# An RNN feeding an LSTM on one core: LSTM step 1's recurrent product in fp16 halves, and the first TensorE instructions in another order

## The reference

```python
x = x + rnn(x, h0=cond_1024)    # h = tanh(h @ Wh + x_t @ Wx + b)
x = x + lstm(x, h0=cond_1024)   # a = x_t @ Wx + h @ Wh + b, 2048 columns: i, f, o, g
                                # c = sigmoid(f)*c + sigmoid(i)*tanh(g);  h = sigmoid(o)*tanh(c)
```

## Time and profile before

| | |
|---|---|
| median of 3 runs | 835.24 us |
| the profiled execution's own time | 836.42 us |
| its span in the trace | 834.6 us |
| TensorE (PE) busy | 823.8 us, 99% |
| VectorE (DVE) busy | 651.4 us, 78% |
| ScalarE (ACT) busy | 608.1 us, 73% |
| GpSimd (POOL) busy | 336.1 us, 40% |

### The profile page before, as it was taken

The page is one execution under the profiler, slowest core; times in us unless marked ns, Lnnn a source line. Parts: engine busy times, 40 slices in busy tenths (PEclk is TensorE's granted clock), DMA queues, the critical chain, the costliest instruction groups (busy, mean ns, idle before and its releaser), DMA issues.

```text
span 834.6 us, 52074 instructions
## 1 busy us (share of the span) xinstructions
PE 823.8 (99%) x22610; PEld 613.4 (73%) x22610; DVE 651.4 (78%) x1797; ACT 608.1 (73%) x1632; POOL 336.1 (40%) x693
## 2 busy tenths in 40 slices
PE   8999999999999999999999999999999999999997
PEld 5556555677777777777777777777777777777786
DVE  4798778877988878878787887878878787767764
ACT  3986576776777677777877778787787878777752
POOL 1422466845544344343434434343343434333320
PEclk9999999999999999999999999999999999999999
DMA  8711101110011111111111111111111101010001
GB/s 304 257 53 28 29 16 29 29 29 23 11 29 30 29 36 30 34 42 38 47 30 34 25 42 41 35 45 35 30 29 42 42 21 37 17 32 23 13 11 28
DMA packets 54580, 36.21 MB, mean 43 GB/s; under 512 B 9788, under 2 KB 52944, under 8 KB 53072
## 3 DMA queue, kind: packets, MB, share of 16 engines
q1 hardware_dynamic: 54096, 32.78, 14.2%
q10 hardware_dynamic: 256, 0.11, 0.0%
HBM read 19.21 MB, written 8.39 MB: 33 GB/s over the span
## 4 chain that ended last, share of the span: by engine, by line
PE 92%; DVE 3%; DMA 2%; issue 1%; ACT 1%; SPq 0%; POOL 0%; ACTq 0%; DVEq 0%; POOLq 0%
PE ps_l L1631 36%; PE ps_l L1726 29%; PE ps_r L1854 9%; PE ps_l L1673 4%; PE ps_pk L1837 3%; PE ps_r L1874 2%; PE ps_end L1837 2%; PE ps_l L1645 2%; DMA whl_raw<-in_L_cond_Wh 2%; PE ps_l L1665 1%; PE ps_r L1785 1%; PE ps_r L1796 1%; DMA wxr_raw<-in_L_cond_Wx 1%; PE ps_l L1618 0%; PE ps_l L1608 0%
## 5 line engine op out<-in xcount | busy, mean ns | idle before, releaser
L598 POOL TENSOR_TENSOR xb<-xb,h_l 128x128 f32<-128x128 f32 x127 | 58.2, 458 | 370.2 <-DVE h_lo L1437 368.0
L1726 PE MATMUL ps_l<-whl_raw,wxl_raw 128*32 128x256 f16 x3816 | 132.0, 273 | 0.0
L1631 PE MATMUL ps_l<-whl_hi,hT_hi 128*32 128x512 f16 x1888 | 122.6, 379 | 0.3 <-DVE hT_hi L1421 0.3
L1631 PE MATMUL ps_l<-whl_hi,hT_lo 128*32 128x512 f16 x1888 | 122.7, 379 | 0.0
L1631 PE MATMUL ps_l<-whl_lo,hT_hi 128*32 128x512 f16 x1888 | 122.5, 379 | 0.0
L1726 PE MATMUL ps_l<-wxl_hi,wxl_raw 128*32 128x256 f16 x2544 | 116.0, 273 | 0.0
L1726 PEld LDWEIGHTS ps_l<-whl_raw,wxl_raw 128*32 128x32 f16 x3816 | 102.2, 97 | 2.5 <-issue 0.4
L1631 PEld LDWEIGHTS ps_l<-whl_hi,hT_lo 128*32 128x32 f16 x1888 | 50.9, 97 | 51.1
L1631 PEld LDWEIGHTS ps_l<-whl_lo,hT_hi 128*32 128x32 f16 x1888 | 50.9, 97 | 51.1
L1009 ACT ACTIVATE gates<-ps_l,g_products 128x256 f32<-128x256 f32 x115 | 54.0, 469 | 41.8 <-PE ps_l L1631 41.6
L1726 PEld LDWEIGHTS ps_l<-wxl_hi,wxl_raw 128*32 128x32 f16 x2544 | 68.6, 97 | 17.5 <-issue 0.2
(11 more groups left out here) (265 smaller groups left out, 1929.6 us busy)
## 6 DMA issues: line engine op xcount, KB each, us to landing
xb<-in_x SPq DMA_DIRECT2D x128, 64.0 KB, 2.1
out<-xb SPq DMA_DIRECT2D x124, 64.0 KB, 1.9
whl_raw<-wxl_lo SPq DMA_DIRECT2D x160, 32.0 KB, 2.3
whl_raw<-in_L_cond_Wh SPq DMA_DIRECT2D x4, 1024.0 KB, 6.4
wxl_raw<-in_L_cond_Wx SPq DMA_DIRECT2D x4, 1024.0 KB, 7.0
wxr_raw<-in_L_cond_Wx SPq DMA_DIRECT2D x1, 1024.0 KB, 6.3
whr_raw<-in_L_cond_Wh SPq DMA_DIRECT2D x1, 1024.0 KB, 8.4
wxl_raw<-in_L_cond_b SPq DMA_DIRECT2D x1, 256.0 KB, 3.5
```

What stands on the lines that cost most here:

```text
L598: nc.gpsimd.tensor_tensor(xb[g % NX][:, t, :], xb[g % NX][:, t, :], h_l[s % 2][:, :], ALU.add).then_inc(out_done, 1)
L1631: last = nc.tensor.matmul(ps_l[s % 4][quarter(j), :], (hT_hi, hT_lo)[h_part][:, k, :], gate_slice(whl[w_part][k], j), start=False, stop=(h ...
L1726: last = nc.tensor.matmul(at[quarter(j), :], stationary, weights[:, j, :, :], start=False, stop=(y_part == 1 and k == 1), skip_group_check ...
```

## The change

LSTM step 1's recurrent product goes from float32 to fp16 halves (N0 from 2 to 1). With it `hidden(0)` writes halves; step 1's bias seed becomes the scaled one, as a second `seed_l` in ScalarE's tick 6; its input is scaled (`y_scale(0)` takes three steps, 128 x 384); the scale is taken off again at its gates. Its three groups of products stand in the order high-high, low hidden times high weights, high hidden times low weights, and the last group waits for each chunk of low halves by itself. TensorE's list begins with fourteen fills in a row; the bias products stand behind them, three of the four behind RNN input product 0. In tick 4 `turn_peaks` stands behind RNN input product 5 and `spread_peaks` behind `step_0_recurrent`. No other table or loop is touched.

```diff
--- before.py
+++ after.py
@@ -18,7 +18,7 @@
 NX = 8
 
 
-N0 = 2
+N0 = 1
 S1 = 5
 G1 = S1 // TG
 
@@ -761,7 +761,7 @@
 
 
             act.wait_ge(bias_mm, 1)
-            nc.scalar.activation(bias_r, ps_l[2][:, 0:P], ACT.Copy).then_inc(bias_done, 1)
+            nc.scalar.activation(bias_r, ps_pk[:, 0:P], ACT.Copy).then_inc(bias_done, 1)
 
             def bias_of_l():
                 act.wait_ge(bias_mm, 2)
@@ -1136,7 +1136,8 @@
                 if k in Y_SCALE_AT:
                     y_scale(Y_SCALE_AT[k])
                 if k == LAG - 1:
-                    seed_l(N0)
+                    for s in range(N0, 3):
+                        seed_l(s)
                 for of, chunk in W_HIGH_LATE_AT.get(k, []):
                     weight_high(of, chunk)
                 if k < LAG and k in R_HIGH_AT:
@@ -1602,8 +1603,8 @@
 
             def step_1_input(k):
 
-                pe.wait_ge(bias_done, 2)
-                pe.wait_ge(yT_done, 2)
+                pe.wait_ge(l_seeded, 1)
+                pe.wait_ge(y_scaled, 1)
                 for j in range(J):
                     last = nc.tensor.matmul(ps_l[1][quarter(j), :], yT[0][:, k, 1, :], gate_slice(wxl_raw[k], j),
                                             start=False, stop=False, skip_group_check=True)
@@ -1621,17 +1622,19 @@
                     return
                 m = s + 1 - N0
                 if m == 1:
-                    pe.wait_ge(w_split[OF_H], J)
+                    pe.wait_ge(w_high[OF_H], J)
                 pe.wait_ge(lstm_hT_hi, m)
                 for h_part, w_part in parts:
                     if h_part == 1:
                         pe.wait_ge(lstm_hT_lo, m)
                     for k in range(J):
+                        if m == 1 and w_part == 1:
+                            pe.wait_ge(w_split[OF_H], k + 1)
                         for j in range(J):
                             last = nc.tensor.matmul(ps_l[s % 4][quarter(j), :], (hT_hi, hT_lo)[h_part][:, k, :],
                                                     gate_slice(whl[w_part][k], j), start=False,
-                                                    stop=(h_part == 1 and k == J - 1), skip_group_check=True)
-                if parts[-1] == (1, 0):
+                                                    stop=((h_part, w_part) == parts[-1] and (1, 0) in parts and k == J - 1), skip_group_check=True)
+                if (1, 0) in parts:
                     last.then_inc(lstm_mm, 1)
 
             def recurrent_halves(s):
@@ -1907,39 +1910,34 @@
                 return last
 
             pe.wait_ge(ident_done, 1)
-            fill(ps_l[3], 3)
-            fill(ps_l[0], 2)
-            fill(ps_end, 1)
+            fill(ps_l[3], 4)
+            fill(ps_l[0], 4)
+            fill(ps_end, 2)
+            fill(ps_l[2], 4).then_inc(banks_written, 1)
             pe.wait_ge(spread_j_done, 1)
             pe.wait_ge(s_bias_r, DMA)
-            nc.tensor.matmul(ps_l[2][:, 0:P], spread_j, bias_rows_r, start=True, stop=True).then_inc(bias_mm, 1)
-
-            for r in (0, 1):
-                nc.tensor.matmul(ps_r[r][:, 0:P], spread_j, bias_rows_r, start=True, stop=True)
-            pe.wait_ge(s_bias_l, DMA)
-            nc.tensor.matmul(ps_l[1][:, :], spread_j, bias_rows_l, start=True, stop=True).then_inc(bias_mm, 1)
-            pe.wait_ge(bias_done, 1)
-            fill(ps_l[2], 6).then_inc(banks_written, 1)
+            nc.tensor.matmul(ps_r[0][:, 0:P], spread_j, bias_rows_r, start=True, stop=True)
             product_r(0)
             for k in range(END):
                 if k - LAG == S1:
                     recurrent_l(S1, ((0, 0), (0, 1)))
-                elif 1 <= k - LAG < S3:
+                elif k - LAG == 1:
+                    recurrent_l(1, ((0, 0), (1, 0), (0, 1)))
+                elif 1 < k - LAG < S3:
                     recurrent_l(k - LAG)
                 elif S3 <= k - LAG:
                     recurrent_halves(k - LAG)
                 if k == LAG - 1:
                     step_0_input(0)
                 if k == 0:
-                    fill(ps_pk, 2)
+                    nc.tensor.matmul(ps_pk[:, 0:P], spread_j, bias_rows_r, start=True, stop=True).then_inc(bias_mm, 1)
+                    nc.tensor.matmul(ps_r[1][:, 0:P], spread_j, bias_rows_r, start=True, stop=True)
+                    pe.wait_ge(s_bias_l, DMA)
+                    nc.tensor.matmul(ps_l[1][:, :], spread_j, bias_rows_l, start=True, stop=True).then_inc(bias_mm, 1)
                 if k < LAG:
                     recurrent_r(k)
                 if k == LAG - 1:
                     step_0_input(1)
-                if k == SCALE_AT[OF_H]:
-                    pe.wait_ge(w_peaked[OF_H], J)
-                    pe.wait_ge(r_step, 1)
-                    turn_peaks(EXCHANGE[OF_H], slice(0, J))
                 if k == SCALE_AT[OF_X]:
                     pe.wait_ge(w_peaked[OF_X], J)
                     pe.wait_ge(x_peaked, BATCHES[0][1])
@@ -1958,14 +1956,19 @@
                 if k < LAG:
                     next_product_r(k + 1)
                 if k == SCALE_AT[OF_H]:
-                    spread_peaks(EXCHANGE[OF_H], J)
+                    pe.wait_ge(w_peaked[OF_H], J)
+                    pe.wait_ge(r_step, 1)
+                    turn_peaks(EXCHANGE[OF_H], slice(0, J))
                 if k == R_SCALE_AT:
+                    pe.wait_ge(bias_done, 1)
                     pe.wait_ge(r_peaked, 2)
                     turn_peaks(EXCHANGE_R, slice(R_PEAK, R_PEAK + 2))
                 if k - 1 == R_SCALE_AT:
                     spread_peaks(EXCHANGE_R, 2)
                 if k in STEP_0_AT:
                     step_0_recurrent(STEP_0_AT[k])
+                if k == SCALE_AT[OF_H]:
+                    spread_peaks(EXCHANGE[OF_H], J)
                 if k == LAG - 1:
                     step_0_input(2)
                     step_1_input(0)
@@ -1975,9 +1978,9 @@
                     step_0_input(3)
                     step_1_input(3)
 
-                if N0 <= k - LAG + 1 < S1:
+                if 2 <= k - LAG + 1 < S1:
                     product_f32(k - LAG + 1, (2, 3))
-                if N0 <= k - LAG + 2 < S1:
+                if 2 <= k - LAG + 2 < S1:
                     product_f32(k - LAG + 2, (0, 1))
                 if k - LAG == S1:
                     product_l(S1 + 1, ((0, 0),))
```

## The result

The changed kernel takes 837.04 us (median of 15 runs, 836.64 to 838.58), the kernel before 835.93 us in the same comparison (15 runs). The ratio is 1.0014, 95% interval 1.0007 to 1.0020: about 1.1 us slower, where 1.0 us was forecast, and less than the 0.2% that would count as a change. The median itself lies above the forecast 836.2 us, mostly because the kernel before has 835.93 us in this comparison and 835.24 us in the three runs that the forecast started from. The profiled execution has a span of 835.6 us (before 834.6).

The account below looks back on a forecast made before the run. TensorE, busy 99% of the span, bounds the kernel. Late operands delay step 2 by 0.78 us and `turn_peaks` by another 0.22: +1.00 us on 835.24 gives 836.2 us, own bounds 835.9 to 836.5, range 834.3 to 837.4 us.

Parts of the forecast that it names:

- The place in TensorE's list decides: An event of the first 75 us counts by its shift of TensorE's list, one to one: +1.00 us at 56.6 us.
- The front counts as nothing: First instructions: RNN's first steps begin 1 to 1.6 us earlier, counted as nothing; ScalarE idles 1.42 us before chunk 2.
- rival C: Front: clock falls to 1.2 GHz in new gaps, products from 24.58 us slow; about 837.7 us; chance 0.09.
- the gap that the prediction named: TensorE idle from about 22.4 us until the product at 24.58 us: 2.2 us in one piece.
- Tick 4 gains 0 to 0.17 us: Tick 4's exchange: TensorE 0.87 us ahead, but the DMA for `step_0_input(2)`, landing at 35.61 us, takes back all but 0.1.
- Rival A: VectorE not late at chunk 3 and step 2, so 0.83 + 0.1 us stay: 834.3 us; chance 0.15.
- ScalarE 0.48 us later at step 0's gates: Tick 6: a seed adds 0.61 us, `y_scale(0)` 0.10, less 0.23 gained; gates of step 0 at 42.00 us.
- VectorE 0.73 us more, 1.21 us late: Tick 7: `hidden(0)` takes 1.41 instead of 0.68 us; with ScalarE's 0.48 everything behind is 1.21 us later.
- 0.65 us inside step 1: Step 1's last group: TensorE waits 0.65 us for `weight_low` of chunk 3, ending at 47.34 us.
- step 2 at 53.78 us: LSTM step 2's product waits for hT_hi at 53.74 us, beginning at 53.78 instead of 53.00 us: +0.78 us.
- The 0.3 us ahead of RNN product 8: Behind step 1: RNN product 8 waits 0.3 us for VectorE's turn, ready at 51.30 us.
- The 0.22 us ahead of `turn_peaks`: Behind step 2's products, ending at 56.37 us: `turn_peaks` waits another 0.22 us for a peak ready at 56.55 us.

Follow-up runs that it names:

- o_fill: Kernel before with the new order alone (step 1 in float32) and 22 fills instead of 14: 834.87 us, ratio 0.9990.
- o_only: Kernel before with the new order alone (fourteen fills first, bias products later, tick 4's exchange behind the products), step 1 in float32: 835.34 us, ratio 0.9994.
- h_only: Kernel before with step 1's halves alone; first instructions and tick 4 stay: 836.79 us, ratio 1.0016.
- a_fill: Changed kernel with 22 fills in a row instead of 14: 836.97 us, ratio 1.0008 to the kernel before.
- a_peak: Changed kernel with the peak of the third group of x on ScalarE in tick 7 instead of VectorE: 836.17 us, ratio 1.0006 to before.
- a_group: Changed kernel with step 1's groups in the old order and one wait for all four low chunks ahead: 840.20 us, ratio 1.0054 to before.
- a_best2: Changed kernel, input chunk 0's bound in tick 7, late x peaks behind step 1's hidden state, half a high part behind its cell tanh: 837.38 us.

## Why the prediction was right

*The place in TensorE's list decides.* Right: 0.77 us at step 3 and 0.98 us at the end of the list, 1.0 us in the span and 1.1 us in the ratio. That it is just 1.0 us is in part luck. Where the sum was made, at `turn_peaks`, the shift is 0.74 us (56.33 against 55.59 us) and not 1.00; terms that were off both ways are listed below, and the last 0.2 us came behind the side work, where nothing was forecast.

*The time itself.* The sum was 836.2 us, 835.9 to 836.5 us within its own bounds, and 837.04 us was measured, outside these bounds and inside the stated 834.3 to 837.4 us. Of the 0.84 us 0.69 are the kernel before, which is 835.93 us in this comparison.

*The front counts as nothing.* Right in the sum, and its cover was what the prediction named: 1.41 us of ScalarE's idle time ahead of chunk 2 are left. But a clock's fall as in rival C came about, behind the gap ahead of RNN product 0. The prediction had eight bias and fill products gone from there and did not ask what fills the time until the weights land. The count is off too: the change takes three of the four bias products from there (six of eight records) and makes the fills two more. The fall was not in the gap that the prediction named: that one was 0.81 us, not 2.2. The Trainium skill, "TensorE: Matmul & The Clock Gate", section "Why this matters for your kernels", warns only of idle gaps that are longer than any in these fronts. The trace goes beyond it: 0.71 us of idle time end 2 us ahead of a clock of 0.50, and the measurement decides.

*Tick 4 gains 0 to 0.17 us.* Too small, and for a wrong reason. `step_0_input(2)` began at 34.95 us, well before 35.6 us, which the prediction had called a sign of being wrong; its chunk had landed at 34.5 us. Rival A, to which that sign pointed, did not follow, since VectorE was late. In the profiles this chunk lands anywhere from 31.7 us (`o_fill`) to 35.6 us (before). `o_only` kept 0.49 us up to step 3. In the changed kernel it is worth at most 1.20 - 0.85 = 0.35 us (`h_only` against changed).

*ScalarE 0.48 us later at step 0's gates.* The added 0.10 and 0.61 us are as forecast (0.60 us for 384 columns, 1.29 us for two seeds). That the new seed costs `step_1_input` nothing held in this profile; in `a_fill` TensorE waited 0.57 us for it. The absolute place, 41.81 us, is 0.29 us later than before, since ScalarE was 0.42 us earlier at the tanh of RNN step 5 (29.59 against 30.01 us), not 0.23.

*VectorE 0.73 us more, 1.21 us late.* 1.41 us as forecast; 0.99 us late at chunk 3. The difference is ScalarE's 0.2 us.

*The waits.* 0.65 us inside step 1 was 0.60 (the prediction's own 46.73 and 47.34 us give 0.61); step 2 at 53.78 us was 53.53, with 0.60 us of waiting for 0.71. The 0.3 us ahead of RNN product 8 did not come, since the idle time of 0.35 us ahead of its turn went. The 0.22 us ahead of `turn_peaks` came: from step 2's product to it are 2.80 us instead of 2.59, so 0.21 us. The experiments show the cause: the halves alone cost it, 1.2 us of useless work on VectorE costs the same, and 2.1 us less takes it away.

*What was not in the sum.* Between step 3 and the end of the list another 0.2 us were lost. Such distances differ by up to 0.9 us between profiles of these kernels (772.9 to 773.8 us from step 3 to the end of the span), so it can't be told from scatter.

## What to carry to other kernels

On an engine that is 99% busy, cheaper work pays only if what feeds it keeps its margin. Read the margin of the next few operands first: here 0.47 us at step 2, against 0.83 us saved and 1.2 us put on the lists that make the operands. And when work is pulled forward from ahead of a DMA's landing, look at the idle time it leaves: in 49 of 90 executions with that idle time the mean clock was under 0.998, and in 7 of 32 with useless products in its place. Last, choose the zero of a comparison so that the engine under study can't move it: a zero that TensorE itself delayed made `a_peak` look 0.5 us better than it was.

## What the hardware did that was not expected

Behind fourteen dense fills and a wait of 0.71 us on TensorE the clock stood at 0.50 from about 10.9 to 14.3 us, while TensorE was busy; after 2.26 us (`a_group`) it was at 0.50 from 10 to 17 us throughout. One wait of 1.23 us (`a_best2`) had no such fall. The landing of a 1 MB weight chunk after its issue varied from 4.9 to 7.1 us between executions at the same place in the list (first input chunk). The exchange moved by up to 2.3 us between profiles, more than most of the effects studied; not all of that is the DMA, since in the two latest (`a_peak`, `a_group`) ScalarE did not wait for the last two recurrent chunks at all.
